# First layer of a decoder from a serial loop to an unrolled pipeline of slots, and other weight loads

## Chip, cores and metric

The kernel runs on one core of a Trainium2 chip, in one launch, with one program. The metric is the device time of an execution in microseconds (us): 1825.73 us as the median of three runs (1823.53 to 1825.94). The engines are TensorE (PE), VectorE (DVE), ScalarE (ACT), GpSimd (POOL), and SyncE (SP), which here only starts transfers (DMAs). Each has a program of its own. They meet at semaphores: `x.wait_ge(sem, n)` holds an engine until the count is n, and `.then_inc(sem, 1)` raises it when an instruction is done.

## What is computed

A decoder of two layers on x of shape (16, 128, 256): B = 16 batches, 128 rows, width 256, fp32, with a context of the same shape. Each part adds its result to its input and normalises the sum. Cut to the order of parts and to the first layer's mathematics:

```python
def bitlinear(x, w):                     # ternary weights, rows rounded to 8 bits
    sw = 1 / clip(mean(abs(w)), 1e-5);  wq = clip(round(w * sw), -1, 1) / sw
    sx = 127 / clip(max(abs(x), -1), 1e-5);  xq = clip(round(x * sx), -128, 127) / sx
    return xq @ wq.T

# layer 0
q, k, v = (bitlinear(x, w).heads(16) for w in (w_q, w_k, w_v))        # 16 heads of 16
x1 = layernorm(x + bitlinear(softmax(causal(q @ k.T / 4)) @ v, w_o))
# cross attention: the 128 rows are channels, 16 heads of 8, over 256 positions
q = rope(conv1x1(x1, wq, bq)); k = rope(conv1x1(ctx, wk, bk)); v = conv1x1(ctx, wv, bv)
x2 = layernorm(x1 + conv1x1(softmax(q.T @ k / sqrt(8)) @ v, wo, bo))  # scores 256 x 256 a head
# top 2 of 8 experts per row: three linear steps 256 -> 512 -> 512 -> 256 with gelu
x3 = layernorm(x2 + experts(x2))
# layer 1: latent causal self-attention, cross attention of 8 heads,
#          retrieval of 8 of 512 rows with a gated MLP; a layernorm after each
```

## The kernel before

`program` runs its stages one after the other: `prepare_weights` (0 to 44.1 us in the profile), `first_layer_attentions` (44.1 to 768.3), `route_tokens` (to about 795), `run_experts` (to about 1130), `second_layer_attentions` (to about 1560) and `retrieve_and_gate` (to the end at 1820.6). The change is in the first layer, in routing and experts, and a little in the preparing stage.

**How an attention is tiled.** Scores are made twice. Queries on partitions: a bank of PSUM (128 x 512, fp32) is filled by `query_scores` with the mask (L389, one matmul of 512 columns) and then by a product with a *stack* (L396 for the cross attention, two matmuls of 256 columns; for the own attention four of 128), and DVE reduces it to two negated maxima (`reduce_maxima`, L452). Keys on partitions: `key_scores` (mask L404, product L411) fills a bank with the maxima already subtracted, and ACT makes exponentials of it into one of the tiles `probs` (L910). Then PE multiplies with the values (`weigh_values` L425 for the own attention, `weigh_shared` L441 for the cross attention, one group per four exponential tiles). A batch has 4 banks of its own attention and 16 of the cross attention, each made both ways: 20 score banks and 20 key banks.

**A stack** is a tile of bf16 pieces of q and k. The fp32 numbers are split into three bf16 parts (`split_parts`: for the cross queries on DVE, for the cross keys and q/k of the own attention on POOL), and SP copies the parts into the rows of the stack: six DMAs a side for the cross attention (`stack_side`, L377), ten or so for the own attention (`stack_parts`, L364 to L367). The maxima get there too, split in two parts (L459, L461), turned by PE and laid by DMAs of ACT's queue.

**Order.** Everything is double-buffered by batch parity, `probs` has PROBS = 8 tiles, and there are two stacks of each kind. `run_steps` (L528) unrolls the first two and last four steps and runs the others in a hardware loop, two steps a pass. Step k on PE, written out by hand: the 4 own score banks of batch k+2, the 16 cross score banks of batch k+1, then the 4 own key banks of k+2 with the products of its values, then the 16 cross key banks of k+1 with its value products. Between them stand the small steps: of batch k (spreading the sums, y, x2, logits L806/L1096), of batch k+2 (cross key product L746/L747, cross query product, heads L726, o L732) and of batch k+3 (q, k, v L692, L754). DVE, ACT, POOL and SP have steps of the same form. SP's order in a step is: context of k+3, the reciprocals of k (L653), cross keys' stack of k+2, store of x2 of k, the own stack of k+3, x of k+4, cross queries' stack of k+2.

**Numbers around it.** DVE's steps named in the trace are: rounding of the rows (`quantise_rows`, L490 to L501; the last, L501, is for the heads), `normalise_heads` (L470), moments (L481 on), the rotation of the cross queries and keys (L1068 and neighbours; POOL adds the halves, L999), the scaling of the values (L1033), the cross sum (L1086).

**Weights of the experts.** W1, W2 and W3 of an expert are 0.5, 1 and 0.5 MB. At the start of the first layer ACT's queue loads W1 of all eight experts. In routing SP loads W2 and W3 of the first AHEAD = 4 experts (L1147), and in `run_experts` those of expert n + 4 in front of tile n of its loop, where it also starts what follows.

**Preparing stage.** The rows of ones in the stacks are written by SP's DMAs (L219): four for the own stacks and eight, four for each stack, for the cross stacks. They are the last of that stage.

Of the kernel before, what the change touches and what calls it, by code (L numbers as in the profile page):

```python
# [110 lines left out]
def prepare_weights(nc, d, t, ps):  # L111

    ctx = ExitStack()
    with ctx:
# [86 lines left out]
        def _(sp):  # L201
# [12 lines left out]
            for att in (SELF0, CROSS0):  # L214
                for u in range(2):
                    for g in range(0, att.groups, 4):

                        rows = t[f"stack_{att.name}"][u][att.rows:att.rows + 2]
# [7 lines left out]
        def _(pool):  # L226
# [5 lines left out]
            for u in range(2):  # L232
                pool.memset(t["stack_cross0"][u][0:CROSS0.rows, :, :, :].bitcast(F32), 0.0)
# [121 lines left out]
def stack_parts(sp, att, stack, parts, made, b, arrived):  # L355

    known = -1
    for n, (a, c) in enumerate(att.terms):
        if max(a, c) > known:
            known = max(a, c)  # L360
            sp.wait_ge(made, 3 * b + known + 1)
        rows = stack[n * att.width:(n + 1) * att.width, :, :]
        if a == c:
            sp.dma_start(rows, parts[:, a, :]).then_inc(arrived, 16)  # L364
        else:
            sp.dma_start(rows[:, :, 0:D], parts[:, a, 0:D]).then_inc(arrived, 16)
            sp.dma_start(rows[:, :, D:2 * D], parts[:, c, D:2 * D]).then_inc(arrived, 16)  # L367
# [96 lines left out]
def normalise_heads(dve, att, out, rden, result):  # L464

    by_bank = out.rearrange("p (g j c) -> p j g c", j=2, c=32)
    order = result.rearrange("p (j g c) -> p j g c", j=2, c=att.width)
    sums = rden[:, 0:2 * att.groups].rearrange("p (j g) -> p j g", j=2)
    for j in range(2):
        dve.reciprocal(sums[:, j], by_bank[:, j, :, att.width])  # L470
    dve.drain()
    for j in range(2):
        ins = dve.tensor_tensor(order[:, j], by_bank[:, j, :, 0:att.width],
                                sums[:, j].unsqueeze(2).broadcast_to([P, att.groups, att.width]), ALU.mult)
    return ins


# [10 lines left out]
def quantise_rows(dve, x, q, whole, rounded):  # L488
# [9 lines left out]
    dve.drain()  # L498
    dve.tensor_scalar(whole, x, q[:, 2:3], ROUND, ALU.mult, ALU.add)
# [3 lines left out]

KEYBANKS, PROBS = 2, 8  # L510


def half(i, u, ahead):

    return i + (u + ahead) // 2


def inside(b):

    return type(b) is not int or 0 <= b < B  # L520


def after_first(b):

    return type(b) is not int or b > 0


def run_steps(engine, first, step):  # L528

    first()  # L530
    for k in (-2, -1):
# [2122 lines left out]
```

## Time and profile before

| what | us |
|---|---|
| median of the runs | 1825.73 |
| the profiled execution | 1822.41 |
| its span in the trace | 1820.6 |
| preparing, to the first layer's start | 44.1 |
| first layer's attentions, 44.1 to 768.3 | 724.2 |
| routing, 768.3 to about 795 | 27 |
| experts, about 795 to 1130 | 335 |
| second layer's attentions, about 1130 to 1560 | 430 |
| retrieval and MLP, about 1560 to the end | 261 |

Over the span the page gives PE 1453.8 us busy (80%), DVE 999.8 (55%), ACT 609.2 (33%) and POOL 366.7 (20%). These shares are means over stages with different limits; for this change the first layer's own stretch counts, of which PE is busy 561.7 us. Its granted clock is 0.93 over the whole first layer and 1.00 in the middle of it.

### The profile page before, as it was taken

To read this page: it belongs to the slowest core of one execution; us is meant where nothing else is said; L and a number is where in the kernel's file an instruction comes from. 1 tells how busy PE (TensorE), PEld (TensorE's weight loads), DVE (VectorE), ACT (ScalarE), POOL (GpSimd) and SP (SyncE) were. 2 spreads that over 40 slices of the span, in tenths; PEclk is the share of its full clock that TensorE was granted. 3 is DMA by queue.
4 is the path that set the end of the run, shared out by engine and by line. 5 is a ranking of instruction groups with operands and counts; after the bars stand their busy time and mean duration, and the time that the engine had idled before them with its cause. 6 is when DMAs were issued, how large, how long until landed. Compare 5 with 4: busy or idle time off the path is not lost. (4 is left out here: it accounts for less than half of the span.)

```text
span 1820.6 us, 29862 instructions
## 1 busy us (share of the span) xinstructions
PE 1453.8 (80%) x9331; PEld 863.5 (47%) x9331; DVE 999.8 (55%) x2735; ACT 609.2 (33%) x1389; POOL 366.7 (20%) x507
## 2 busy tenths in 40 slices
PE   2478888878888787539999996558888886799997
PEld 1234444444444443226566564335565553466664
DVE  5256666666666665242222222357887763467775
ACT  0133333334333332212232232225566543233231
POOL 1211112112111110011111111445555430000000
PEclk9589999999999998769999998678999998799999
DMA  4323222222223221054111111384455420200000
GB/s 127 104 47 51 47 45 50 48 48 50 53 52 53 47 40 22 29 193 133 36 35 31 34 33 36 76 186 98 115 116 120 104 64 19 74 1 12 12 1 24
DMA packets 165279, 112.22 MB, mean 62 GB/s; under 512 B 32682, under 2 KB 155818, under 8 KB 165040
## 3 DMA queue, kind: packets, MB, share of 16 engines
q1 hardware_dynamic: 150256, 95.09, 23.1%
q0 software_dynamic: 3408, 9.31, 2.0%
q10 hardware_dynamic: 11504, 6.46, 1.3%
q8 instruction: 55, 0.90, 0.2%
q14 instruction: 56, 0.46, 0.1%
HBM read 46.48 MB, written 12.45 MB: 32 GB/s over the span
## 5 line engine op out<-in xcount | busy, mean ns | idle before, releaser
L910 ACT ACTIVATE first_probs<-pair 128x512 f32<-128x512 f32 x320 | 177.6, 595 | 131.3 <-PE pair L411 129.0
L452 DVE TENSOR_REDUCE first_negmax_x<-bank 128x2 f32<-128x512 f32 x256 | 169.0, 685 | 64.0 <-PE bank L396 57.7
L396 PE MATMUL bank<-kept_stack_cross 96*128 96x256 bf16 x768 | 156.1, 286 | 11.4 <-DMA kept_stack_cross<-second_parts_x_q 9.5
L1891 ACT ACTIVATE second_probs<-pair 128x512 f32<-128x512 f32 x192 | 113.7, 598 | 130.7 <-PE pair L411 115.5
L411 PE MATMUL pair<-kept_stack_cross 98*128 98x256 bf16 x768 | 151.3, 280 | 1.5 <-DMA kept_stack_cross<-second_rows_x 1.0
L389 PE MATMUL bank<-kept_mask_q,kept_ident 128*128 128x512 bf16 x256 | 104.8, 409 | 57.4 <-DMA kept_stack_cross<-first_parts_x_q 31.6
L1405 PE MATMUL pair<-kept_w,experts_hidden_t 128*128 x312 | 140.3, 592 | 0.0
L452 DVE TENSOR_REDUCE second_negmax_x<-bank 128x2 f32<-128x512 f32 x128 | 88.6, 692 | 60.4 <-PE bank L396 52.5
L396 PEld LDWEIGHTS bank<-kept_stack_cross 96*128 96x128 bf16 x768 | 75.7, 103 | 75.5 <-issue 26.2
L404 PE MATMUL pair<-kept_mask_t,kept_ident 128*128 128x512 bf16 x256 | 100.8, 394 | 11.7 <-ACT first_probs L910 8.3
L1446 ACT ACTIVATE experts_hidden_t<-bank,kept_b 128x128 f32<-128x128 f32 x156 | 44.6, 368 | 183.2 <-PE bank L1380 183.2
L411 PEld LDWEIGHTS pair<-kept_stack_cross 98*128 98x128 bf16 x768 | 75.5, 101 | 42.8 <-issue 4.9
L1405 PEld LDWEIGHTS pair<-kept_w,experts_hidden_t 128*128 128x128 f32 x312 | 59.2, 190 | 74.1 <-issue 74.1
L1360 POOL DMA_INDIRECT experts_expert_rows<-x_mid,kept_row_of x39 | 37.1, 950 | 273.1 <-PE bank L1372 246.0
L1483 DVE COPY experts_hidden<-pair 128x512 f32<-128x512 f32 x39 | 27.0, 692 | 107.5 <-PE pair L1405 107.5
L1396 PE MATMUL bank<-kept_w,experts_expert_rows_t 128*128 x156 | 75.5, 607 | 1.4 <-DVE experts_expert_rows_t L1471 1.2
L1414 PE MATMUL pair<-kept_w,experts_hidden_t 128*128 x312 | 73.9, 380 | 1.4 <-ACT experts_hidden_t L1454 1.4
L389 PEld LDWEIGHTS bank<-kept_mask_q,kept_ident 128*128 128x128 bf16 x256 | 25.1, 98 | 99.7 <-DVE first_negmax_x L452 58.5
L441 PE MATMUL pair<-first_probs,kept_v_cross 128*32 128x256 f32 x1024 | 70.0, 392 | 1.5 <-ACT first_probs L910 1.5
L389 PE MATMUL bank<-kept_causal_q,kept_ident 128*128 128x512 bf16 x128 | 52.3, 409 | 22.3 <-DMA kept_stack_self<-first_parts_a 13.3
L999 POOL TENSOR_TENSOR first_full_x_k<-first_cosd_k,first_sind_k 128x256 f32<-128x256 f32 x16 | 11.6, 724 | 288.6 <-DVE first_sind_k L1068 288.6
L1477 DVE COPY experts_hidden<-bank 128x512 f32<-128x512 f32 x39 | 27.0, 692 | 64.8 <-PE bank L1396 64.8
(430 smaller groups left out, 2965.7 us busy)
## 6 DMA issues: line engine op xcount, KB each, us to landing
kept_stack_self<-first_parts_a SPq DMA_DIRECT2D x128, 64.0 KB, 3.1
kept_w<-in_L_ffn_W SPq DMA_DIRECT2D x8, 1024.0 KB, 7.1
kept_stack_self<-second_parts_a SPq DMA_DIRECT2D x128, 64.0 KB, 3.4
kept_stack_cross<-first_parts_x_k SPq DMA_DIRECT2D x96, 64.0 KB
kept_stack_cross<-first_parts_x_q SPq DMA_DIRECT2D x96, 64.0 KB
kept_stack_cross<-second_parts_x_k SPq DMA_DIRECT2D x96, 64.0 KB, 2.5
kept_stack_cross<-second_parts_x_q SPq DMA_DIRECT2D x96, 64.0 KB
expert_out<-experts_expert_done SPq DMA_DIRECT2D x39, 128.0 KB, 1.8
```

The costliest lines, as they stand in the source:

```text
L389: pe.matmul(bank[:, :], ident16, mask, start=True, stop=False, skip_group_check=True)
L396: mm = pe.matmul(out, q, k, start=mask is None, stop=True, skip_group_check=True)
L404: pe.matmul(bank[:, :], ident16, mask, start=True, stop=False, skip_group_check=True)
L411: mm = pe.matmul(out, k, q, start=mask is None, stop=True, skip_group_check=True)
L441: mm = pe.matmul(out[j * 32:(j + 1) * 32, at * D:(at + 1) * D], values[:, 2 * k + at, a, j, :], probs[j][:, k * D:(k + 1) * D], start=(a = ...
L452: return dve.tensor_reduce(negmax[:, 2 * n:2 * n + 2], bank[:, :].rearrange("p (m t) -> p m t", t=D), AX.X, ALU.max, negate=True)
L910: act.activation(probs[(phase + n) % PROBS][:, :], key_bank[n % KEYBANKS][:, :], ACT.Exp, scale=att.scale).then_inc(probs_made, 1)
L1396: mm = pe.matmul(layer1_bank[:, :], rows_t[n % 2][:, k, :], t["w1"][:, bass.ds(expert, 1), k, :].rearrange("p a f -> p (a f)"), start=(k = ...
L1405: mm = pe.matmul(layer2_bank[:, :], hidden1_t[n % 2][:, k, :], t["w2"][:, bass.ds(expert, 1), k, :].rearrange("p a f -> p (a f)"), start=( ...
L1414: mm = pe.matmul(layer3_bank[:, 0:D], hidden2_t[n % 2][:, k, :], t["w3"][:, bass.ds(expert, 1), k, :].rearrange("p a f -> p (a f)"), start ...
L1446: ins = act.activation(hidden1_t[n % 2][:, k, :], turn1_bank[:, k * P:(k + 1) * P], ACT.Gelu, bias=t["b12"][:, k, bass.ds(expert, 1)])
L1891: act.activation(probs[i % PROBS][:, :], key_bank[i % 2][:, :], ACT.Exp, scale=att.scale).then_inc(probs_made, 1)
```

## The change

**First layer.** The hardware loop and its steps are gone. Every engine's program is unrolled over slots from -33 to 404; a batch's work starts 20 slots after the one before it. A table gives each kind of step its slot relative to the batch's first: own scores in 0 to 3, cross scores in 39 and from 44 on, own keys from 9, cross keys in 65 to 68 and from 73 on, the store of x2 in 99, the logits kept in 104. A slot holds at most one score bank and one key bank, of whatever batches are due. In each slot PE takes the score bank, the key bank, and then the small steps due. DVE drains its pipe at the end of each slot.

There are three cross stacks in place of two, with semaphores of their own for each side; three buffers of x (`x0`) and of the context, four of x1, and 12 tiles of probabilities. The cross queries are split by POOL, as the keys were already. The own stack is copied part by part (`stack_part`) in three slots. The reciprocals' DMA goes from SP's to ACT's queue. `normalise_heads` is one reciprocal and one product in place of two each. The row scales and the rounding of the rows are steps of their own.

**Preparing.** The ones' rows of the third cross stack are four DMAs more.

**Experts.** The loads of W1 at the first layer's start are gone. `load_expert` loads W1, W2 and W3 of an expert, AHEAD is 3, and SP waits for the first turned rows of a tile ahead of its loop of loads and stores.

**Second layer.** Its `WINDOW`, `batch_at` and `Lane` become the class `Slots`, shared with the first layer, with the same numbers.

```diff
+class Slots:
+    def batch_at(self, slot, offset):
+        b, rest = divmod(slot - offset, self.window)
+        return b if rest == 0 and 0 <= b < B else None
...
+        slots = Slots(20)
+        OWN_SCORES, CROSS_SCORES, OWN_KEYS, CROSS_KEYS = 0, ((39, 1), (44, 15)), 9, ((65, 4), (73, 12))
...
+        LOAD_CONTEXT, MAKE_CROSS_K, ROTATE_K, SPLIT_KEYS, STACK_KEYS = 5, 11, 12, 15, 25
+        MAKE_CROSS_Q, ROTATE_Q, SPLIT_QUERIES, STACK_QUERIES = 29, 29, 30, 31
...
         @block.sync
         def _(sp):
-                if inside(k + 3):
-                    stack_self(i, u, 3)
-                if inside(k + 4):
-                    load_rows(i, u, 4)
-                if inside(k + 2):
-                    stack_cross(i, u, 2, 0)
...
+            for s in SLOTS:
...
+                if (b := slots.batch_at(s, STACK_QUERIES)) is not None:
+                    stack_cross(b, 0)
+                if (b := slots.batch_at(s, STACK_FIRST)) is not None:
+                    stack_self(b, 0)
...
         @block.tensor
         def _(pe):
+            def cross_scores(b, n):
+                i = query_lane.index("cross", b, n)
+                if n == 0:
+                    pe.wait_ge(stack_q[b % 3], SIDE * (b // 3 + 1))
+                    pe.wait_ge(stack_k[b % 3], SIDE * (b // 3 + 1))
+                if i >= 2:
+                    pe.wait_ge(reduced, i - 1)
+                query_scores(pe, CROSS0, score_bank[i % 2], t["stack_cross0"][b % 3], n, ident16[:, :], mask_q).then_inc(scored, 1)
...
-            for e in range(NE):
-                act.dma_start(t["w1"][:, e, :, :], d["L0_ffn_W1"][e].rearrange("(k p) f -> p k f", p=P)).then_inc(t["expert_loaded"][e], 16)
...
 def load_expert(queue, d, t, e):
-    weights = (("L0_ffn_W2", "w2"), ("L0_ffn_W3", "w3"))
+    weights = (("L0_ffn_W1", "w1"), ("L0_ffn_W2", "w2"), ("L0_ffn_W3", "w3"))
...
-AHEAD, IOTAS = 4, 5
+AHEAD, IOTAS = 3, 5
...
+            sp.wait_ge(rows_turned, 1)
             for n in range(TILES):
                 if n + AHEAD < NE:
                     load_expert(sp, d, t, n + AHEAD)
```

PE in the middle of the first layer. Before, among the cross score banks (`bank_2`, `bank_3`) of one batch, with the cross key product of another in `bank_1`; key banks are `pair_1` and its like and do not come here. REGISTER_ALU is the loop's counting.

```order
L389 MATMUL bank_2<-kept_mask_q,kept_ident16 128x512
L396 MATMUL bank_2<-kept_stack_cross0_1 128x256 x2
L769 REGISTER_ALU
L389 MATMUL bank_3<-kept_mask_q,kept_ident16 128x512
L396 MATMUL bank_3<-kept_stack_cross0_1 128x256 x2
L745 REGISTER_ALU
L746 MATMUL bank_1<-first_kv_0,kept_xw_t 128x256
L747 MATMUL bank_1<-first_kv_0,kept_xrot_t 128x256
```

After, cross score banks of one batch, with own key banks of another between them:

```order
L386 MATMUL bank_2<-kept_mask_q,kept_ident16 128x512
L393 MATMUL bank_2<-kept_stack_cross0_1 128x256 x2
L401 MATMUL pair_1<-kept_causal_t,kept_ident16 128x512
L408 MATMUL pair_1<-kept_stack_self0_1 128x128 x4
L782 MATMUL bank_1<-first_x1_0,kept_xw_t 128x256
L783 MATMUL bank_1<-first_x1_0,kept_xrot_t 128x256
L386 MATMUL bank_3<-kept_mask_q,kept_ident16 128x512
L393 MATMUL bank_3<-kept_stack_cross0_1 128x256 x2
L401 MATMUL pair_1<-kept_causal_t,kept_ident16 128x512
L408 MATMUL pair_1<-kept_stack_self0_1 128x128 x4
```

Between two score banks stands a key bank now, where two score banks stood side by side.

DVE at the end of a batch's cross maxima. Before, all 16 reductions (L452) are done, and the splitting of the maxima, the cross sum of another batch and its moments follow without a reduction between them:

```order
L452 TENSOR_REDUCE first_negmax_x<-bank_3 128x2
L459 CAST first_two_x<-first_negmax_x 128x32
L461 TENSOR_TENSOR first_two_x<-first_negmax_x,first_two_x 128x32
L1086 SCALAR_TENSOR_TENSOR first_sum_x<-pair_0,kept_bo,first_x1_1 128x256
L481 BN_STATS first_stats_x<-first_sum_x 128x6
L483 BN_AGGR first_stats_x<-first_stats_x 128x2
L485 TENSOR_SCALAR first_stats_x<-first_stats_x 128x1
```

After, slot 15 of a batch's 20 (cross sum L1117, moments, row scales L473 to L1032 of a later batch), with the next slot's reduction behind it:

```order
L449 TENSOR_REDUCE first_negmax_x<-bank_2 128x2
L1117 SCALAR_TENSOR_TENSOR first_sum_x<-pair_0,kept_bo,first_x1_3 128x256
L464 BN_STATS first_stats_x<-first_sum_x 128x6
L466 BN_AGGR first_stats_x<-first_stats_x 128x2
L468 TENSOR_SCALAR first_stats_x<-first_stats_x 128x1
L473 TENSOR_REDUCE first_qs<-first_x0_1 128x1
L475 TENSOR_SCALAR first_qs<-first_qs 128x1
L477 RECIPROCAL first_qs<-first_qs 128x1
L478 TENSOR_SCALAR first_qs<-first_qs 128x1
L480 TENSOR_SCALAR first_qs<-first_qs 128x1
L1032 TENSOR_SCALAR first_s4<-kept_mw4,first_qs 128x4
L449 TENSOR_REDUCE first_negmax_x<-bank_3 128x2
```

Reductions, which were 16 in a row, now have the other steps between them.

SP, whose queue orders the stacks' DMAs. Before, the queries' stack of a batch, then the context, the reciprocals, the keys' stack of the next and the store stand ahead of the own stack:

```order
L377 DMA kept_stack_cross0_0<-first_parts_x_q 8x16x256 x6
L631 DMA first_kv_0<-in_ctx_2048 128x1x256
L653 DMA first_heads_x<-first_recips 8x16x32
L377 DMA kept_stack_cross0_1<-first_parts_x_k 8x16x256 x6
L658 ISA
L658 DMA x_mid<-first_x2_1 128x256
L361 ISA
L364 DMA kept_stack_self0_0<-first_parts_a 16x8x512
```

After, the own stack stands right behind the queries' stack:

```order
L631 DMA x_mid<-first_x2_1 128x256
L615 DMA first_kv_1<-in_ctx_2048 128x1x256
L374 DMA kept_stack_cross0_0<-first_parts_x_k 8x16x256 x6
L610 DMA first_x0_0<-in_x 128x1x256
L374 DMA kept_stack_cross0_0<-first_parts_x_q 8x16x256 x6
L360 DMA kept_stack_self0_1<-first_parts_a 16x8x512
L362 DMA kept_stack_self0_1<-first_parts_a 16x8x256
L364 DMA kept_stack_self0_1<-first_parts_a 16x8x256
```

The reciprocals' DMA is no longer in this queue, and both sides of one batch's cross stack come before the own stack of a later batch.

## Rows read from the trace of the kernel before

**Rows 1.** Windows: length; busy us (x count) of PE, PEld, DVE, ACT, POOL; clock, DMA, GB/s.

```profile
44.10:768.30 724.20, 561.71 (x4416) 304.55 (x4416) 421.39 (x1066) 247.70 (x512) 130.01 (x176) 0.93 0.26 49
327.10:367.20 40.10, 32.37 (x273) 17.90 (x272) 26.27 (x67) 14.98 (x32) 8.12 (x11) 1.00 0.28 49
1340.00:1380.00 40.00, 35.00 (x350) 23.88 (x347) 32.20 (x79) 24.16 (x54) 21.80 (x31) 1.00 0.52 117
```

**Rows 2.** Waits of PE, 285 to 605 us: total us, times, longest.

```profile
PE bank L389 <- DMA kept_stack_cross<-first_parts_x_q: 16.0, 8, 2.1
PE bank L389 <- DVE first_negmax_x L452: 13.2, 38, 0.6
```

**Rows 3.** Line L1096 (ns min/median/max, first and last start), and ACT's last exponentials in the timeline.

```profile
L1096 DVEq FUSED_REGOPS  x12: 57/64/64, 165.9 to 617.2; - x12
...
750.89 1.09 ACT L910 ACTIVATE first_probs<-pair 128x512 f32<-128x512 f32 x2 [0.57 <-PE pair L411]
```

**Rows 4.** Timeline of PE, one batch in the middle: start us, us, instruction.

```profile
508.33 1.07 PE L441 MATMUL pair<-first_probs,kept_v_cross 128*32 128x256 f32 x16
...
509.34 0.39 PE L389 MATMUL bank<-kept_causal_q,kept_ident 128*128 128x512 bf16 x1
...
509.79 0.38 PE L389 MATMUL bank<-kept_causal_q,kept_ident 128*128 128x512 bf16 x1
...
514.79 0.60 PE L746 MATMUL bank<-first_kv,kept_xw_t 128*128 128x256 f32 x2
...
515.22 0.59 PE L747 MATMUL bank<-first_kv,kept_xrot_t 128*128 128x256 f32 x2
```

**Rows 5.** Timeline of DVE, same stretch; last, line L501 over the whole layer.

```profile
486.29 0.18 DVE L459 CAST first_two_x<-first_negmax_x 128x32 bf16<-128x32 f32 x1
...
486.65 0.48 DVE L1086 SCALAR_TENSOR_TENSOR first_sum_x<-pair,kept_bo,first_x 128x256 f32<-128x256 f32 x1
...
488.27 0.48 DVE L1033 TENSOR_SCALAR kept_v_self<-bank,first_s 128x256 f32<-128x256 f32 x1 [0.15 <-PE bank L692]
...
492.19 0.28 DVE L470 RECIPROCAL first_rden_a<-bank 128x8 f32<-128x8 f32 x2 [2.92 <-PE bank L726]
...
493.12 0.42 DVE L490 TENSOR_REDUCE first_qo<-first_heads_a 128x1 f32<-128x256 f32 x1
...
494.37 0.35 DVE L499 TENSOR_SCALAR first_whole_o<-first_heads_a,first_qo 128x256 f32<-128x256 f32 x1
...
517.68 3.47 DVE L452 TENSOR_REDUCE first_negmax_x<-bank 128x2 f32<-128x512 f32 x5
...
L501 DVE TENSOR_SCALAR first_oq<-first_whole_o x16: 294/586/662, 81.5 to 699.3; 128x256 bf16<-128x256 f32 x16
```

**Rows 6.** Timeline at the first own stack, and at a keys' rotation with its stack.

```profile
61.62 0.61 PE L389 MATMUL bank<-kept_causal_q,kept_ident 128*128 128x512 bf16 x1 [11.84 <-DMA kept_stack_self<-first_parts_a]
...
79.95 2.62 SPq L364 DMA_DIRECT2D kept_stack_self<-first_parts_a  x2
...
89.97 0.61 PE L389 MATMUL bank<-kept_causal_q,kept_ident 128*128 128x512 bf16 x1 [1.51 <-DMA kept_stack_self<-first_parts_a]
...
517.29 0.47 DVE L1068 SCALAR_TENSOR_TENSOR first_sind_k<-bank,kept_bqk_rot,kept_sin 128x256 f32<-128x256 f32 x1
...
519.35 3.88 SPq L377 DMA_DIRECT2D kept_stack_cross<-first_parts_x_k  x6
```

**Rows 7.** Timeline at the experts' start, and landing times of L1147 (796 to 870 us).

```profile
803.21 0.69 PE L1372 MATMUL bank<-kept_ident,experts_expert_rows 128*128 128x128 f32 x2 [8.94 <-DMA experts_expert_rows<-x_mid,kept_row_of]
...
826.39 1.66 SPq L1147 DMA_DIRECT2D kept_w<-in_L_ffn_W  x2
...
833.65 1.88 PE L1396 MATMUL bank<-kept_w,experts_expert_rows_t 128*128 x4
...
DMA to landing us min/median/max: 5.7/6.7/7.7
```

**Rows 8.** Timeline at the end of the preparing stage, SP.

```profile
30.44 4.89 SPq L219 DMA_DIRECT2D kept_stack_cross<-prepare_ones_row_bf  x8
```

More of the change, by code:

```diff
@@ L231, in _ @@
             pool.memset(ones_row[:, :, :], 1.0).then_inc(constants_made, 1)
-            for u in range(2):
-                pool.memset(t["stack_cross0"][u][0:CROSS0.rows, :, :, :].bitcast(F32), 0.0)
+            for stack in t["stack_cross0"]:
+                pool.memset(stack[0:CROSS0.rows, :, :, :].bitcast(F32), 0.0)
             pool.sem_inc(t["weights_ready"], 1)
@@ new lines, in stack_self, with stack_cross @@
+            def stack_self(b, part):
+                sp.wait_ge(parts_a_made, 3 * b + part + 1)
+                if part == 0 and b >= 2:
+                    sp.wait_ge(key_scored, key_lane.index("own", b - 2, SELF0.banks - 1) + 1)
+                stack_part(sp, SELF0, t["stack_self0"][b % 2], parts_a, part, stack_a[b % 2])
+            def stack_cross(b, side):
+                if b >= 3:
+                    sp.wait_ge(key_scored, key_lane.index("cross", b - 3, CROSS0.banks - 1) + 1)
+                stack_side(sp, CROSS0, t["stack_cross0"][b % 3], parts_x[side], (parts_q_made, parts_k_made)[side], b, side,
+                           (stack_q, stack_k)[side][b % 3])
@@ L723, in turn_out, with own_values @@
+            def own_values(b):
+                i = key_lane.index("own", b, 0)
+                if b >= 1:
+                    pe.wait_ge(sum_a_made, b)
+                pe.wait_ge(v_copied, b + 1)
+                pe.wait_ge(probs_made, i + GROUP)
+                weigh_values(pe, SELF0, bank_a, [probs[(i + n) % RING] for n in range(GROUP)], t["v_self0"][b % 2], 0).then_inc(probs_used, 1)
             def turn_out(b):
@@ L1021, in _ @@
-            run_steps(pool, first, step)
+            for s in SLOTS:
+                if (b := slots.batch_at(s, ROOT_A)) is not None:
+                    root(stats_a, var_a_made, rstd_a_made, b)
+                if (b := slots.batch_at(s, ROOT_X)) is not None:
+                    root(stats_x, var_x_made, rstd_x_made, b)
+                if (b := slots.batch_at(s, SPLIT_QUERIES)) is not None:
+                    split_cross(b, 0)
+                if (b := slots.batch_at(s, SPLIT_SELF)) is not None:
+                    split_self(b)
+                if (b := slots.batch_at(s, SPLIT_KEYS)) is not None:
+                    split_cross(b, 1)
```

983 lines of the change are left out of this document (489 added, 494 removed).

## Prediction

> **What bounds the kernel now.** I read the views from the whole down to one batch. First the windows by stage [rows 1]: the first layer's attentions take 724.2 of 1820.6 us, TensorE (PE) is busy for 561.7 of them. In the middle, at a granted clock of 1.00, PE is busy 32.4 of 40.1 us, VectorE (DVE) 26.3, ScalarE (ACT) 15.0, GpSimd (POOL) 8.1, so no engine is full. The period of a batch is in [rows 3]: the same register step once a batch, 12 times from 165.9 to 617.2, so 451.3 / 11 = 41.0 us. Second, who makes PE wait [rows 2]: over eight batches 16.0 us for the cross stack's queries and 13.2 us for the maxima of DVE (these two are the longest of a list that adds to about 57 us, 7.1 a batch). The loop is serial by kind of work: 20 score banks in a row, paced by DVE's reductions, then 20 key banks paced by exponentials. What ends a wait is always the engine that has a different 20 us of the batch to itself. So this stage is bound by order, not by an engine. The reader should see a period of 41 above a PE sum of 32.
>
> **The steady state after.** A slot holds one score bank and one key bank. PE's price of a bank is at most the 509.79 - 509.34 = 0.45 us from start to start in [rows 4], and at least its 1024 columns at 2.4 GHz (granted clock 1.00), 0.427; I take 0.435, so 0.87 a slot and 17.4 a batch. Five groups of value products at 1.07 plus a gap of 0.03 are 5.5. Side steps: each product of two 256-column fp32 matmuls steps 515.22 - 514.79 = 0.43 [rows 4]; keys, queries, spread and y are two of these each (3.5), values, turned rows, q/k/v, o, logits and the small transposes add 3.5 by their columns. PE's floor is 17.4 + 5.5 + 7.0 = 29.9 us a batch.
>
> DVE does not disappear beside that. Its steps go to slots, and slots 15 to 19 of each 20 get most: five reductions at 3.47 / 5 = 0.69 (3.5), cross sum and moments 488.27 - 0.15 - 486.65 = 1.5, row scales 494.37 - 493.12 + 0.2 = 1.45, rounding 0.7, the split of the maxima 0.36 + 0.15, normalising heads 493.12 - 492.19 = 0.9 (0.75 with one instruction fewer of each kind), x2 0.4, head scales 1.45 [rows 5]. With a drain at each slot's end, which the trace of before doesn't show here (I put it at 0.09, half of the 0.18 that lies between a step's end and the next start at 486.47 to 486.65; bounds 0 and 0.18), that is 10.5 us, while PE has 6.0 us of work there. PE may run two slots ahead (two score banks), so the loop that sets the period is: PE from slot 2 to slot 15 (13 slots at 0.87, four value groups 4.4, side steps 6.2: 21.9 us), one score until DVE may start (0.435 and a signal of 0.2, 0.64), DVE over slots 15 to 19 (10.5), one reduction and its signal (0.69 + 0.05 = 0.74) until PE's slot 2: **33.8 us**. The steps of DVE in a whole batch add to 28.7 us, counted from start to start in the same way (its busy time now is 26.27 / 40.1 of 41.0, 26.9).
>
> Two things can lengthen it. Some DVE steps have two prices: the rounding of the heads took 0.29 at best, 0.66 at worst and 0.59 in the middle [rows 5], which I read as POOL's work beside them, and the change moves splits by POOL to slots 10 to 16. I add 0.7 for two such steps (bounds 0 and the 2 us of the splits): **34.5 us**. The other is the stack of the next batch's own keys, on SP behind the queries' stack: the cross query's products with the steps ahead of them 1.8 (0.86 the products, the rest an estimate), rotation, POOL's split and six DMAs 519.35 + 3.88 - 517.29 = 5.9 after a start 0.6 later, then the ten DMAs and their landing 89.97 - 79.95 = 10.0 [rows 6], with a reciprocal's DMA ahead on DVE (1.1) 19.5 us from slot 9 to slot 20. PE has 17.4 us there and 19.5 with the stall above, so it just fits.
>
> The Trainium skill speaks against one part of this. The queries' split (five DVE steps, about 2 us a batch) goes from DVE to POOL, and "Perfetto Trace Analysis", section "Optimizing Scalar/DVE Operations", says that moving work between DVE and GpSimd might not help, since they share a port; "SBUF — State Buffer", section "SBUF: two separate sides", calls it an exclusive lock in which the loser blocks for the whole instruction. The step of two prices above agrees with it. Taken in full it would give the 2 us back each batch, and the time would be 1723 + 13 x 2 = 1749, which is within B below.
>
> **Fill and drain.** Own scores of batch 0 start at 61.62 now [rows 6]. The third cross stack adds 4 of the ones' DMAs to the queue that ends the preparing stage, 4 x 4.89 / 8 = 2.4 us [rows 8]; the eight loads of W1 that ran in front of the first x are gone, which no row here prices; I put it at 2 us back (bounds 0 and 3.9, half of a landing of 7.7 [rows 7]). So slot 0 is at 61.7. Batch 1's rows are now turned before batch 0's keys (slot 8, not after the values), so its stack is there at about 82 where batch 1's scores began at 89.97. Then each window is slots 0 to 8 (about 10, later 12.5 us) plus the 19.5 us chain: slot 40 at 111.5, slot 60 at 141, slot 80 at 173. From there eleven windows at 34.5 end at slot 300, 552.5. Drain: slots 300 to 319 without a next batch to prepare 31.5; to 339 without own banks 24.5; to 359 with 31 banks 21; the last 21 key banks, five value groups and a laying of reciprocals 21; then the tail as now, 768.3 - 752.0 = 16.3 [rows 1, 3]. That gives 667, so the first layer saves **101 us** (bounds: period 31.5 or 37 over some 13 windows, -39 and +33; fill and drain 10 either way).
>
> **Routing and experts.** Before, SP loads the fourth expert in front of the first gather, and PE waits 8.94 us for rows until 803.21 [rows 7]. Now three experts of 2 MB (as many bytes as four of 1.5) are loaded in routing and SP waits for the first turned rows, so the gather should land 3.8 us earlier (bounds 0 and 5). Queued behind that wait on SP are expert 3's load (three tiles of 826.39 to 833.65, 22 us, away from its use) and the stores, which wait longer anyway. Experts 4 to 7 are then loaded 826.39 to 833.65 = 7.3 us ahead of their tile. The last DMA of 1.5 MB landed 7.7 us at most after its issue [rows 7], 7.2 after the first; 0.5 MB more is a third of the transfer, so 8.6: 1.4 us late, and since a tile's load hangs on the tile before last, it is paid twice, 2.8 us (bounds 0 and 9). Sum -1. The second layer and retrieval are unchanged but for names.
>
> Against the profiled span: 1820.6 - 101.3 - 1 = 1718.3. The profiled execution's time was 1.8 above its span (1822.4), and 3.3 below the median (1825.7), so 1718.3 + 5.1 = **1723 us**.
>
> **Rivals.**
> A. PE-bound: DVE's long slots are absorbed, because its two-slot lag covers more or the steps overlap better, and the period is 31.5. For it: DVE's total of 28.7 is under PE's 29.9. Against: 10.5 us in one stretch. Slots 80 to 300 save 33: 1690.
> B. The slots leave small waits everywhere, or the port takes the 2 us back. For it: the second layer already runs in slots and PE is still idle 5.0 of 40 us there [rows 1], DVE busy 32.2. Five DVE steps beside POOL's splits at 0.66 - 0.29 = 0.37 more each are 1.9 [rows 5]. Period 36.5 to 37: 1723 + 11 x 2.3 + 5 = 1753.
> C. Late weights: five experts 6 us late each, if a load of 2 MB lands 13 to 14 us after its issue, not 8.6. 1753 as well, but from the experts.
> D. Slower than before: SP holds the order. STACK_QUERIES stands before the own stack and waits for POOL, which waits for DVE's rotation, which stands behind a reciprocal that waits for a DMA. If this ring takes over 26 us instead of 19.5, the window is over 41 and the deeper pipeline (137 slots a batch, against about four steps) is all loss. It decides at a window of 34.5 + 101 / 15 = 41.2; at 43, 1850. Against: every wait in it has a measured price, and SP's 25 DMAs of a batch at 3.88 / 6 = 0.65 [rows 6] are 16 us of 34.
> E. The order changes and nothing comes of it, since fill and drain of the deeper pipeline take what the period gives. My fill ends only 12 us later than the same number of batches at full pace would, so I hold it for unlikely.
>
> **Chances.** My forecast (period 33.5 to 35.5) 0.48, A 0.14, B 0.25, C 0.05, D 0.05, E 0.03. The range takes in A and B: 1690 to 1760. A measurement of this kernel can tell about 0.2% from no change; the four first cases are faster, 0.92; E is shared, 0.02 same and 0.01 slower, and D makes slower 0.06.
>
> **What would show it.** Right: starts of a batch's first own score 34 to 35 us apart in the middle; PE's waits for the queries' stack gone; a new wait of PE for the maxima, about 2 us in all, at slots 18 to 2, after a DVE stretch without a gap; batch 0's first cross score near 110; end of the layer's last logits near 667; gather's wait about 5 us; up to 1.5 us of wait for W at tiles 4 and 6. Wrong: a period under 32.5 (DVE is not in the loop), or PE waiting mainly for DMAs of the own stack (the SP chain is the loop), or waits on products one slot old.

## The result and the profile after

| | before | after |
|---|---|---|
| median of the runs, us | 1824.63 (1819.99 to 1825.94, 4 runs) | 1769.39 (1762.19 to 1778.06, 4 runs) |
| ratio, 95% interval | | 0.970 (0.966 to 0.975) |
| profiled span, us | 1820.6 | 1765.9 |
| PE's first own score to its last logits product | 61.6 to 768 | 60.6 to 710 |

The change is faster by 55 us, where 101 to 103 were forecast; the forecast of 1723 us is 46 too low, and the time lies outside the range that ended at 1760. The windows below answer to [rows 1]: length, busy us (x count) of PE, PEld, DVE, ACT and POOL, then the granted clock of PE, the DMA share and GB/s. They are the whole first layer, one batch in the middle, the eleven batches from slot 80 to 300, the drain from slot 300 on, and the experts.

```profile
60.60:710.20 649.60, 525.79 (x4406) 318.64 (x4406) 393.60 (x943) 251.34 (x508) 174.19 (x252) 0.94 0.37 49
320.50:357.10 36.60, 31.12 (x279) 19.26 (x278) 24.40 (x61) 15.81 (x32) 11.13 (x16) 1.00 0.45 57
175.30:582.00 406.70, 347.33 (x3030) 214.38 (x3031) 266.28 (x645) 172.99 (x350) 122.37 (x176) 0.98 0.42 55
582.00:710.20 128.20, 103.25 (x817) 58.16 (x815) 60.43 (x136) 50.43 (x99) 13.06 (x22) 0.93 0.14 22
740.60:1067.00 326.40, 318.59 (x1170) 189.00 (x1170) 85.24 (x155) 88.91 (x312) 34.55 (x37) 0.98 0.20 64
```

A batch takes 36.6 us in place of 41.0, and PE is idle 5.5 us of it, where the forecast left 34.5 - 29.9 = 4.6. Eleven batches took 406.7 us, 37.0 each. Who makes PE wait there is the view that answers to [rows 2] (nine batches, 211.4 to 545; total us, times, longest):

```profile
PE bank L386 <- DVE first_negmax_x L449: 21.3, 18, 1.8
PE pair L401 <- DMA kept_stack_self<-first_rows_a: 12.4, 8, 1.7
PE bank L386 <- DVE first_negmax_a L447: 8.2, 9, 1.4
PE bank L792 <- issue: 6.6, 9, 0.7
PE bank L685 <- DVE kept_v_self L1043: 1.6, 9, 0.2
```

The wait for the queries' stack, 16.0 us before, is gone, as the change wants it. In its place stand DVE's maxima, which I had forecast (29.5 us in nine batches, 3.3 each), and two waits that I had not: the laid rows of the own maxima (1.4 each) and the cross values' products (0.7). One batch shows the places. The rows are PE's, start us and us: slot 2, the own keys of slot 9, the cross values of slot 13, slot 15, slot 18, and slot 2 of the next batch.

```profile
324.29 0.39 PE L386 MATMUL bank<-kept_causal_q,kept_ident 128*128 128x512 bf16 x1 [0.85 <-DVE first_negmax_a L447]
...
337.00 0.39 PE L401 MATMUL pair<-kept_causal_t,kept_ident 128*128 128x512 bf16 x1 [1.40 <-DMA kept_stack_self<-first_rows_a]
...
345.73 0.68 PE L792 MATMUL bank<-kept_xw_t,first_kv 128*128 128x128 f32 x4 [0.74 <-issue]
...
349.19 0.38 PE L386 MATMUL bank<-kept_mask_q,kept_ident 128*128 128x512 bf16 x1
...
354.20 0.39 PE L386 MATMUL bank<-kept_mask_q,kept_ident 128*128 128x512 bf16 x1 [1.77 <-DVE first_negmax_x L449]
...
360.83 0.39 PE L386 MATMUL bank<-kept_causal_q,kept_ident 128*128 128x512 bf16 x1 [0.86 <-DVE first_negmax_a L447]
```

From slot 2 to slot 15 are 349.19 - 324.29 = 24.9 us, and from there to the next slot 2 are 360.83 - 349.19 = 11.6. The forecast was 21.9 and 11.9.

DVE's timeline in the same batch shows the second part. It is idle before slot 15 (the first row) and then works without a gap to the own maxima of slot 0 (the last row), for which PE waits in slot 2; the row scales (L473 to L1032) and the rounding of the rows (L486, L488) stand in it.

```profile
349.83 0.69 DVE L449 TENSOR_REDUCE first_negmax_x<-bank 128x2 f32<-128x512 f32 x1 [2.25 <-PE bank L393]
...
351.88 0.42 DVE L473 TENSOR_REDUCE first_qs<-first_x 128x1 f32<-128x256 f32 x1
...
360.08 0.69 DVE L447 TENSOR_REDUCE first_negmax_a<-bank 128x4 f32<-128x512 f32 x1
```

**The experts.** Two tiles wait for their weights (L1430, start us, us, and the wait):

```profile
773.11 3.28 PE L1430 MATMUL bank<-kept_w,experts_expert_rows_t 128*128 x4 [1.88 <-DMA kept_w<-in_L_ffn_W]
...
782.88 1.88 PE L1430 MATMUL bank<-kept_w,experts_expert_rows_t 128*128 x4
...
793.18 2.88 PE L1430 MATMUL bank<-kept_w,experts_expert_rows_t 128*128 x4 [2.17 <-DMA kept_w<-in_L_ffn_W]
```

Against the kernel before, the spacings of all other tiles are equal to 0.01 us, and those of tiles 4 and 6 are longer by 3.84 and 4.13. Only 1.88 + 2.17 = 4.1 of these 8.0 us is the wait. The rest follows it: the first product of the late tile takes 3.28 us, the same product one tile later 1.88. That is TensorE at the lower of its two clocks for a part of it: the granted clock is 0.51 from 773.6 to 777.0 us and 0.50 from 794.1 to 797.5.

**Where the 47.6 us of span went.**

| stretch | forecast | measured | difference |
|---|---|---|---|
| start to slot 80 | to 173 | to 175.3 | +2.3 |
| slots 80 to 300 | 379.5 | 406.7 | +27.2 |
| slot 300 to the last logits | 114.5 | 128.2 | +13.7 |
| routing, to the first turned rows | 31.1 | 30.4 | -0.7 |
| experts | 318.4 + 2.8 | 326.4 | +5.2 |
| the rest | 699.0 | 698.9 | -0.1 |

### The profile page after: what moved, and what is told of

It reads as the page before. It is cut to its first block and busy times, and to the rows that moved or that the text cites. A ratio compares the mean times of both kernels' runs of the same rounds, so it can differ in the third digit from the quotient of the medians.

```text
span 1765.9 us, 29494 instructions
## 1 busy us (share of the span) xinstructions
PE 1422.5 (81%) x9331; PEld 878.0 (50%) x9331; DVE 975.9 (55%) x2623; ACT 614.0 (35%) x1389; POOL 418.3 (24%) x588
## 5 line engine op out<-in xcount | busy, mean ns | idle before, releaser
L892 ACT ACTIVATE first_probs<-pair 128x512 f32<-128x512 f32 x320 | 190.3, 597 | 302.6 <-PE pair L408 273.4
L449 DVE TENSOR_REDUCE first_negmax_x<-bank 128x2 f32<-128x512 f32 x256 | 177.0, 692 | 109.5 <-PE bank L393 96.1
L393 PE MATMUL bank<-kept_stack_cross 96*128 96x256 bf16 x768 | 150.4, 277 | 9.7 <-DMA kept_stack_cross<-second_parts_x_q 7.9
L386 PE MATMUL bank<-kept_mask_q,kept_ident 128*128 128x512 bf16 x256 | 99.3, 388 | 35.0 <-DVE first_negmax_x L449 26.8
L386 PE MATMUL bank<-kept_causal_q,kept_ident 128*128 128x512 bf16 x128 | 53.5, 418 | 48.9 <-DMA kept_stack_self<-first_parts_a 24.6
L1430 PE MATMUL bank<-kept_w,experts_expert_rows_t 128*128 x156 | 77.9, 624 | 5.5 <-DMA kept_w<-in_L_ffn_W 4.1
L401 PE MATMUL pair<-kept_causal_t,kept_ident 128*128 128x512 bf16 x128 | 53.0, 414 | 20.0 <-DMA kept_stack_self<-first_rows_a 19.2
L2442 POOL TENSOR_TENSOR retrieve_stats<-retrieve_stats,kept_minus_half 128x1 f32<-128x1 f32 x16 | 8.9, 557 | 251.3 <-DVE retrieve_stats L468 251.3
```

Of the source, the lines that this page charges most:

```text
L386: pe.matmul(bank[:, :], ident16, mask, start=True, stop=False, skip_group_check=True)
L393: mm = pe.matmul(out, q, k, start=mask is None, stop=True, skip_group_check=True)
L401: pe.matmul(bank[:, :], ident16, mask, start=True, stop=False, skip_group_check=True)
L449: return dve.tensor_reduce(negmax[:, 2 * n:2 * n + 2], bank[:, :].rearrange("p (m t) -> p m t", t=D), AX.X, ALU.max, negate=True)
L892: act.activation(probs[i % RING][:, :], key_bank[i % 2][:, :], ACT.Exp, scale=att.scale).then_inc(probs_made, 1)
L1430: mm = pe.matmul(layer1_bank[:, :], rows_t[n % 2][:, k, :], t["w1"][:, bass.ds(expert, 1), k, :].rearrange("p a f -> p (a f)"), start=(k = ...
```

## Experiments

In all of them the period of a batch is read from one instruction that runs once a batch on DVE, the keeping of the logits (L1129 in the changed kernel, 16 times). The periods named are the mean of its first ten spacings, so the middle of the layer; the tenth reaches a little into the drain, and in some kernels is 1 to 2 us shorter than the others. These are the rows of the changed kernel and of three of the experiments, with min/median/max in ns and the first and the last start in us, in the order changed kernel, three edits, own stack first, row scales in slots 10 and 11:

```profile
L1129 DVE TENSOR_TENSOR kept_logits<-pair,kept_bg x16: 155/156/167, 220.3 to 710.0; 128x8 f32<-128x8 f32 x16
L1129 DVE TENSOR_TENSOR kept_logits<-pair,kept_bg x16: 157/159/167, 222.9 to 688.8; 128x8 f32<-128x8 f32 x16
L1129 DVE TENSOR_TENSOR kept_logits<-pair,kept_bg x16: 157/159/167, 218.1 to 682.3; 128x8 f32<-128x8 f32 x16
L1129 DVE TENSOR_TENSOR kept_logits<-pair,kept_bg x16: 156/159/167, 217.2 to 669.8; 128x8 f32<-128x8 f32 x16
```

| kernel | period | half clock a batch | last logits | experts | run, us |
|---|---|---|---|---|---|
| changed kernel | 36.95 | 1.0 | 710.0 | 326.0 | 1769.4 (median of 4) |
| the same, once more | 37.15 | 1.4 | 716.3 | 326.6 | 1781.0 |
| row scales in slots 13, 14 | 35.47 | 1.4 | 695.3 | 325.4 | 1760.2 |
| own maxima in slot 4 | 35.89 | 0.3 | 703.5 | 326.2 | 1768.4 |
| weights one tile earlier | 37.12 | 1.7 | 714.9 | 318.0 | 1769.9 |
| all three | 34.45 | 0 | 688.8 | 318.0 | 1744.5 (median of 4) |
| queries' split on DVE | 37.07 | 1.4 | 717.3 | 330.5 | 1784.9 |
| three, own stack first | 34.42 | 0 | 682.3 | 318.0 | 1740.9 |
| and cross values in slot 14 | 34.33 | 0 | 681.1 | 318.0 | 1737.1 (median of 5) |
| and row scales in slots 10, 11 | 33.35 | 0 | 669.8 | 318.0 | 1722.5 (median of 5) |

"Half clock a batch" is the time at the lower clock in those ten spacings, us a batch. Work of one microsecond takes two there (of the rows at the end of this document the L386 product at 376.12 us is followed by PE's next one at 376.55, that at 378.87 by one at 379.09), so I take half of it off where I compare periods; the changed kernel has then 36.4. The column of the experts runs from the start of the first turned rows to the start of the last product, 0.4 us less than to its end.

**Row scales earlier.** The part of DVE's gapless stretch that could move.

```diff
-        ..., ROW_SCALES, ROUND_ROWS, ... = -33, -25, -24, ...
+        ..., ROW_SCALES, ROUND_ROWS, ... = -33, -27, -26, ...
```

> Changed kernel with the row scales and the rounding of the rows moved two slots earlier on VectorE, from slots 15 and 16 of the 20 to slots 13 and 14, where VectorE waits 2.25 us for TensorE. Loop theory (the period is TensorE's slots 2 to 14, 24.9 us, plus VectorE's stretch from slot 15 to slot 2, 11.7 us): the stretch loses 2.1 us, the period goes from 36.7 to about 34.6 and the first layer gets some 29 us shorter. Rival (another chain, such as SP's stack of the own keys, stands right behind): VectorE's wait goes, a wait for a DMA takes its place, period 36 to 37.

Measured: the period without half clock is 34.8, 1.7 less (spacings without a fall of the clock were 34.0 to 35.4, where the changed kernel has 35.6 to 37.0). PE's waits over nine batches:

```profile
PE pair L401 <- DMA kept_stack_self<-first_rows_a: 12.8, 8, 1.7
PE bank L792 <- issue: 6.7, 9, 0.7
PE bank L386 <- DMA kept_stack_self<-first_parts_a: 5.5, 9, 0.9
PE bank L386 <- DVE first_negmax_x L449: 5.0, 9, 0.7
```

The waits for DVE's maxima fell from 29.5 to 5.9 us (0.9 of it for the own maxima), 2.6 a batch, and a new one of 0.6 a batch for the own stack came up. So DVE's stretch did hold the period. The own stack's wait is not what holds it now: in most batches DVE has no idle time of more than 0.1 us from slot 12, where it waits 0.67 us for the spread sums, to the own maxima of slot 0, 14.6 to 15.2 us later. The stretch has got a new front; the experiment with the cross values in slot 14 shows it. The layer became only 14.6 us shorter, not 29: four of those ten spacings hold a fall of the clock, and the fill has more half clock as well.

**Own maxima earlier.**

```diff
-        OWN_TWO, TURN_OWN_MAXIMA, OWN_ROWS, ... = 3, 5, 5, ...
+        OWN_TWO, TURN_OWN_MAXIMA, OWN_ROWS, ... = 3, 4, 4, ...
-        STORE_ROWS, TURN_X2, COPY_X2, MAKE_LOGITS, KEEP_LOGITS = 99, 101, 101, 103, 104
+        STORE_ROWS, TURN_X2, COPY_X2, MAKE_LOGITS, KEEP_LOGITS = 99, 101, 101, 102, 103
```

> Changed kernel with the own maxima turned and laid in slot 4, not 5; the logits, which share a bank, are made and kept one slot earlier for that. Loop theory: TensorE's wait of 1.6 us at slot 9 for the laid rows of maxima lies inside the loop and goes almost whole, period 36.7 to about 35.2, and the stretches at half clock behind that wait (three in the layer, 1.9 us each) go too: first layer about 25 us shorter. Rival (the wait is slack that hides another chain): period stays at 36 to 37 and the 1.6 us turn up at another wait.

Measured: the wait for the laid rows is gone from the list, and the period without half clock goes from 36.4 to 35.7, 0.7 less where 1.5 was expected. (The spacings without a fall of the clock, the tenth left out, say 0.4: 36.1 in the mean, 36.5 in the changed kernel.) Over nine batches two small waits took its place, besides those that stay:

```profile
PE bank L386 <- DVE first_negmax_x L449: 19.6, 16, 1.8
...
PE bank L782 <- ACT first_full_a L912: 4.0, 9, 0.5
...
PE pair L379 <- DVE kept_logits L1129: 1.5, 8, 0.5
```

These are 5.0 us more in nine batches (0.5 of L782 was there before), or 0.6 of the 1.4 a batch that went. So a part of the wait lay inside the loop, as the theory has it, but 0.4 of it had covered ACT's copy of q and k, and the earlier slot of the logits cost 0.2.

**Weights earlier.**

```diff
-                if n + AHEAD < NE:
-                    load_expert(sp, d, t, n + AHEAD)
+                for e in ((AHEAD, AHEAD + 1) if n == 0 else (n + AHEAD + 1,)):
+                    if e < NE:
+                        load_expert(sp, d, t, e)
```

> Changed kernel with each expert's weights loaded one tile earlier (experts 3 and 4 both behind the first turned rows). Late-weights theory: only tiles 4 and 6 are long, by 3.84 and 4.13 us, of which 4.1 is the wait for weights and the rest half clock behind it; both go, the experts' stage is 8 us shorter, 326 to 318. Rival (4 MB in a row are late themselves or delay the gathers): a gain under 3 us, or a new wait at tile 2 or 3.

Measured: PE from the first turned rows to the last product of the experts takes 318.0 us, not 326.0, with a granted clock of 0.99 in place of 0.98; this is the theory's 8 us to 0.1. The row of the window, to the end of that product:

```profile
745.90:1064.30 318.40, 314.66 (x1170) 187.60 (x1170) 85.31 (x155) 89.16 (x312) 34.80 (x37) 0.99 0.20 65
```

The run as a whole was not faster (1769.9 us). Its first layer, which has the code of the changed kernel, took 5 us more than that kernel's, at more half clock, and the code behind the experts 5 us more too (703.8 for 698.9).

**All three.**

> All three edits together. If the loop theory holds for both, period about 33.1 (TensorE's work alone is 31), first layer 29 + 25 shorter, experts 8 shorter: 1769 - 62 = 1707 us. If another chain stands behind, period 34.5 to 35.5 and 1725 to 1740 us.

Measured: 1744.53 us (median of 4, 1740.73 to 1750.27), 0.957 of the kernel before (0.954 to 0.959). The period is 34.45, not 33.1: the case "another chain stands behind", whose time of 1725 to 1740 us it still misses by 4.5. Nine batches:

```profile
PE bank L386 <- DMA kept_stack_self<-first_parts_a: 10.2, 9, 1.6
PE bank L792 <- issue: 6.6, 9, 0.7
PE bank L386 <- DVE first_negmax_x L449: 4.5, 9, 0.7
PE bank L782 <- ACT first_full_a L912: 4.0, 9, 0.5
```

Own maxima earlier, which was worth 0.7 alone, is worth 0.3 after the row scales (34.8 to 34.45): the wait for the own stack has grown to 1.1 us a batch, and DVE is again without a gap from slot 12 in half of the batches and with 0.2 to 0.5 us of one in the others. With fewer and shorter waits, 1.6 us at the longest, the clock no longer falls in the middle of the layer at all.

**Queries' split on DVE**, the rival of the port, on the changed kernel.

```diff
-                if (b := slots.batch_at(s, SPLIT_QUERIES)) is not None:
-                    split_cross(b, 0)
...
+            def split_queries(b):
+                ...
+                dve.tensor_tensor(full_x[0][:, :], cosd[0][:, :], sind[0][:, :], ALU.add)
+                dve.drain()
+                split_parts(dve, full_x[0][:, :], rest_x[0][:, :], parts_x[0], t["ones_bf"][:, 0:1], parts_q_made)
```

> Changed kernel with the cross queries' sum and split back on VectorE, in slot 10 of the 20, as in the kernel before. Theory (no port cost): VectorE's durations are as before with POOL's share moved, so moving the split to POOL gave the 2 us a batch only where VectorE was short; in slot 10 it is not, period 36 to 37 as now, perhaps 0.5 less since POOL's split of q and k starts earlier. Rival (the port took the 2 us back, as my case B had it): the other VectorE steps get shorter by some 2 us a batch in sum and the period drops to about 35.

Measured: period 37.07 (36.4 without half clock, the same as the changed kernel). The five steps on DVE take 2.4 us a batch there, and DVE's other steps of the layer are together 419.0 us, against 420.8 in the changed kernel (421.5 in its second run): 0.1 us a batch. The rounding steps show how that comes about. In the kernel before L501 took 579 ns for the heads and 294 for the rows on average; in the changed kernel the same two forms are:

```profile
L488 DVE TENSOR_SCALAR first_xq<-first_whole 128x256 bf16<-128x256 f32 x16 | 7.0, 440 | 1.2
...
L488 DVE TENSOR_SCALAR first_oq<-first_whole_o 128x256 bf16<-128x256 f32 x16 | 4.7, 294 | 1.2
```

One form has lost its doubling and the other has got a part of one. In these two kernels and this run the step took 293 to 295 ns each time that no instruction of POOL overlapped it (74 times), and 448 to 1235 ns each time that one did (22 times, 15 of them the heads' step of the kernel before). In the changed kernel it is 4 times of 32, all in the fill. So for this step the cost went where POOL's work went. The Trainium skill ("SBUF — State Buffer", section "SBUF: two separate sides") has the two engines exclude each other on a port; these steps agree with it, but a mechanism that doubles some steps is no price by itself, and here the whole of it was 0.1 us a batch.

**Own stack first**, on top of the three edits.

```diff
-        SPLIT_SELF, STACK_FIRST, STACK_SECOND, STACK_THIRD = -8, -7, -6, -5
+        SPLIT_SELF, STACK_FIRST, STACK_SECOND, STACK_THIRD = -11, -10, -9, -8
-        MAKE_CROSS_Q, ROTATE_Q, SPLIT_QUERIES, STACK_QUERIES = 29, 29, 30, 31
+        MAKE_CROSS_Q, ROTATE_Q, SPLIT_QUERIES, STACK_QUERIES = 29, 29, 30, 33
```

> The version with all three edits, with POOL's split and SP's stack for the own attention ahead of those for the cross queries (own split in slot 9, stack in 10 to 12, queries' stack in 13). Theory (SP's and POOL's chain of the own stack is the next limit): TensorE's 1.1 us of wait a batch for the own stack goes, period 34.4 to 33.3, and the first windows, now 32 us, get 2 to 5 us shorter each. Rival (the queries' stack becomes late in its place): TensorE waits for it at slot 19, period 34 or more.

Measured: the period is 34.42, unchanged. The wait for the own stack is gone, the queries' stack is not late, and 0.8 of its 1.1 us a batch stand at DVE's own maxima now: both of my cases missed that. That wait had been slack beside DVE's stretch. The waits over 315 us:

```profile
PE bank L386 <- DVE first_negmax_a L447: 7.5, 9, 1.1
...
PE bank L386 <- DVE first_negmax_x L449: 5.0, 9, 0.6
```

The layer ends 6.5 us earlier all the same, 4.8 of them already at the first kept logits, so they come from the fill.

**Cross values in slot 14**, on top of that.

```diff
-        MAKE_CROSS_V, COPY_CROSS_V, ... = 53, 53, ...
+        MAKE_CROSS_V, COPY_CROSS_V, ... = 54, 54, ...
```

> As the run before, and the cross values' products in slot 14 in place of 13, since TensorE waits 0.73 us a batch there for VectorE's rotation of the keys. Theory: period 32.6; first layer 15 x 1.8 = 27 us shorter than with the three edits, 1744 - 27 = 1717 us. Rival (the waits are now set by VectorE's stretch, which still has 9.5 us): period 33.5, 1730 us.

Measured: 1737.07 us, 0.954 (0.952 to 0.956), period 34.33. The wait at L792 is gone and the waits for the cross maxima grew from 5.0 to 12.2 us, so it is once more the rival that holds. DVE's timeline tells why. The first row is its last idle time, in slot 12, where it waits for the spread sums; the second follows without a gap, and so does all the work down to the own maxima of slot 0, for which PE waits in slot 2 (0.80 us, until 420.06).

```profile
405.23 0.69 DVE L1113 TENSOR_TENSOR first_heads_x<-first_heads_x,pair 128x512 f32<-128x512 f32 x1 [0.82 <-PE pair L810]
405.84 0.48 DVE L1101 SCALAR_TENSOR_TENSOR first_cosd_k<-bank,kept_bqk,kept_cos 128x256 f32<-128x256 f32 x1
...
419.32 0.69 DVE L447 TENSOR_REDUCE first_negmax_a<-bank 128x4 f32<-128x512 f32 x1
```

By moving the row scales from slot 15 to slot 13 I had made the stretch longer at its front. It now begins in slot 12 and is 14.8 us long, where the changed kernel has 10.9 from slot 15, and every wait of PE behind slot 12 is slack beside it.

**Row scales in slots 10 and 11**, on top of that.

```diff
-        ..., ROW_SCALES, ROUND_ROWS, ... = -33, -27, -26, ...
+        ..., ROW_SCALES, ROUND_ROWS, ... = -33, -30, -29, ...
```

> As the run with the own stack first and the cross values in slot 14, with the row scales and rounding moved on from slots 13 and 14 to slots 10 and 11. In the trace before it VectorE works without a gap from slot 12 (the rotation of the keys, after its wait for the spread sums) to slot 2 of the next batch, and waits 2.5 us in slots 9 to 12. Theory (the loop is still TensorE to VectorE and back, now closed at slot 12): the gapless stretch gets 2.1 us shorter and the period goes from 34.3 to 32.2, at least to TensorE's 31 plus small waits, 32.5; 15 x 1.8 = 27 us less, 1737 to 1710. Rival (VectorE is full anyway): the wait moves to slots 10 to 12, period 34.

Measured: 1722.45 us (median of 5, 1719.52 to 1724.6), 0.945 of the kernel before (0.943 to 0.947), and period 33.35: half of the expected 2.1 us. This is the best version. The waits left over 315 us:

```profile
PE bank L386 <- DVE first_negmax_a L447: 6.5, 9, 1.0
PE bank L782 <- ACT first_full_a L912: 4.5, 10, 0.5
PE bank L386 <- DVE first_negmax_x L449: 3.0, 9, 0.3
```

The cross maxima's waits went from 12.2 to 3.0 us; those for the own maxima hardly moved (7.5 to 6.5). Why they stay was not tried, but DVE's timeline shows where the loop closes now:

```profile
403.62 0.69 DVE L449 TENSOR_REDUCE first_negmax_x<-bank 128x2 f32<-128x512 f32 x1 [1.66 <-PE bank L393]
...
411.81 0.69 DVE L447 TENSOR_REDUCE first_negmax_a<-bank 128x4 f32<-128x512 f32 x1
```

DVE is idle at slot 15 again (1.15 to 1.67 us in ten batches) and mostly without a gap from there to the own maxima of slot 0. This is the loop of the forecast once more: PE takes 23.6 us from slot 2 to slot 15, and the rest of it is 9.6.

**The changed kernel once more.**

> The changed kernel once more, with no edit. In three kernels with the same code behind the experts that part took 668 to 680 us with 122 to 150 us at half clock. Clock theory: it differs as much between two executions of one kernel, so the time moves by 5 to 10 us with the same waits. Rival (it is a trait of a kernel's code): 668 us again and the same stretches at half clock.

Measured: 1780.98 us, 13.3 more than the changed kernel's profiled run. The code behind the experts, the same in both, took 686.5 us in the first profile and 692.4 in this one. The two windows:

```profile
1079.30:1765.80 686.50, 560.45 (x3656) 359.08 (x3656) 441.22 (x1290) 266.91 (x558) 184.51 (x270) 0.92 0.29 68
```

```profile
1086.70:1779.10 692.40, 566.11 (x3625) 362.81 (x3656) 442.73 (x1290) 267.37 (x558) 184.56 (x270) 0.90 0.29 67
```

The waits in the first layer are alike (18.7 and 21.3 us for the cross maxima, 13.0 and 12.4 for the laid rows), but the granted clock of the layer is 0.93 against 0.94, and it ends 6.3 us later. So the same code differs by some 6 us in each of two stages between executions, by where the clock falls. A single run of the experiments above therefore tells 10 us badly, while periods without half clock agree to 0.2 us in the three kernels with this layer (36.4, 36.5, 36.3). This is the clock theory, with 13 us in place of its 5 to 10.

## Why the prediction was wrong

- **What bounds the kernel.** Right: the stage was bound by order; with another order and nearly the same work of PE (31.1 us a batch for 32.4) a batch takes 36.6 us.
- **PE's floor, 29.9.** 31.1 measured (PE busy 31.12 in a batch of 36.6), 1.2 too low. Of this, slots 2 to 14 hold 0.7: 24.9 less the waits 1.40, 0.74 and 0.18 is 22.6, where I had 21.9.
- **The loop PE, DVE, PE.** Its shape was right: DVE's part is 11.6 (forecast 11.9; its steps in slots 15 to 19 take 10.25, where I wrote 10.5 and my own terms add up to 10.7), and taking 2.1 us out of it took 1.7 off the period and nearly all of PE's waits for maxima.
- **The step that failed** is "PE from slot 2 to slot 15: 21.9 us". I summed PE's work there and no wait, and the loop runs through its waits as well. It is 24.9: 1.4 for the laid rows of the own maxima at slot 9 (up to 1.7 in other batches), 0.74 for the rotation before the cross values, 0.18 for v, 0.7 of work. Each of these waits hangs on a chain that starts at PE itself a few slots earlier. The change put turning and use of the own maxima four slots apart, and I never priced this distance. It takes 337.00 - 330.16 = 6.8 us from the turning to the keys; PE was through with what stands between them after 5.4. That makes the period 33.8 + 3.0 - 0.3 = 36.5, which is that batch's. Against the 34.5 of the forecast this is 2.0 a batch, 22 of the 27 us that slots 80 to 300 took too long. What is shown of it: the waits were measured in place, and taking the one at slot 9 away gave 0.4 to 0.7 us of its 1.4, the rest going to waits behind it. That the wait at slot 13 costs its 0.74 in this kernel was not tried by itself; it was taken away only where DVE's longer stretch held the period, and gave 0.1.
- **Port.** I added 0.7 a batch, and B up to 2. Neither is there: 0.1 us a batch.
- **The own stack just fits.** Right: no wait for it in the changed kernel's middle, 0.6 to 1.1 us as soon as the period fell to 35.5 and below, though taking that wait away left the period at 34.4.
- **Clock.** Not in my sum at all. Four of the eleven batches from slot 80 hold a stretch at half clock, 13.6 us in sum. Three of these stretches begin behind a wait of 1.7 us at slot 9, and two of these batches take 38.6 and 38.7 us where their neighbours take 36.5 to 37.1. In all 4 to 7 us of the 27.
- **Fill.** Slot 0 at 60.6 (forecast 61.7, though its own terms, 61.62 + 2.4 - 2, give 62.0), slot 40 at 109.8 (111.5), slot 60 at 143.4 (141), slot 80 at 175.3 (173): right.
- **Drain.** 128.2 for 114.5. The windows took 33.4, 26.9, 24.7, 25.7 and 17.5 us for 31.5, 24.5, 21, 21 and 16.3. Over the whole drain PE waits 7.3 us for laid reciprocals, in three times, and 4.7 for the cross maxima, and the clock is 0.87 in the fourth window. I had priced the drain as work, with one laying of reciprocals and no other wait.
- **Experts.** The wait was right in place and in its kind (tiles 4 and 6, 4.1 us where I had 2.8), but what it brings is twice as much, since half clock follows each. Loading one tile earlier brings it all back.
- **Gather.** Forecast 3.8 us less wait: 8.94 to 5.07. Right.
- **Rivals.** Measured 1769 lies beyond B (1753): B's period of 36.5 to 37 is the one that came, and for the first of its two reasons, small waits in the slots, not for the port; late weights (C, a quarter of its size) and the drain came on top. B had for it that PE is idle 5.0 of 40 us in the second layer's slots, and here it is 5.5 of 36.6; but its price came from the port's steps and it named none of these waits, so that the period met B's is in part luck. My chance of 0.48 for a period of 34.5 was too high, since it was built on a path that had no wait in it.

## What to carry to other kernels

If a period is worked out as a loop over two engines, walk the first engine's part with every semaphore that it passes, and give each the time from its producer to its use; a wait that is nowhere the largest still adds when it lies in the loop. A stretch of the second engine without a gap has a front that moves: work taken from its middle and put just ahead of it can tie it to what stood before (here 10.9 us became 14.8, and the gain stopped at 1.7), so put it ahead of the last place where that engine really waits, which gave 1.0 more. And load early enough that no wait is left at all: here two waits of some 2 us for weights cost 4 us each.

## What the runs showed of the hardware

- After some waits of about 2 us PE was granted half its clock (1.2 for 2.4 GHz) in the work behind: the same L386 product took 0.63 us in place of 0.38, the experts' first product 3.28 in place of 1.88. The length of the wait does not decide it alone. In the ten spacings of the changed kernel the clock fell three times, each behind a wait of 1.67 to 1.70 us at slot 9, and not behind the other six there, of 1.26 to 1.66 us, nor behind any of the nine waits of 1.76 to 1.83 us at slot 18; with all three edits it did not fall behind waits of up to 1.6 us. In the three kernels with no wait above 1.1 us these ten spacings ran at a clock of 1.00 throughout. What else decides it was not looked into. Here are the rows at slot 9 of one batch, a wait of 1.70 us and what follows:

```profile
373.85 0.39 PE L401 MATMUL pair<-kept_causal_t,kept_ident 128*128 128x512 bf16 x1 [1.70 <-DMA kept_stack_self<-first_rows_a]
...
374.31 1.17 PE L782 MATMUL bank<-first_x,kept_xw_t 128*128 128x256 f32 x2
...
376.12 0.63 PE L386 MATMUL bank<-kept_mask_q,kept_ident 128*128 128x512 bf16 x1
...
378.87 0.39 PE L386 MATMUL bank<-kept_mask_q,kept_ident 128*128 128x512 bf16 x1
```

- Two small DMAs of ACT's queue that lay the maxima were issued by 331.19 + 1.33 = 332.5 and let PE go at 337.0, 4.5 us later, while SP's six DMAs of the keys' stack and a load of x were on their way beside them. That they would land sooner without these was not tried. The rows:

```profile
328.83 3.95 SPq L374 DMA_DIRECT2D kept_stack_cross<-first_parts_x_k  x6
...
330.16 0.22 PE L379 MATMUL pair<-kept_ident,first_two_a 128*128 128x128 bf16 x1
...
331.19 1.33 ACTq L350 DMA_DIRECT2D kept_stack_self<-first_rows_a  x2
```
